# Asking for the spread decays in ScalarE's queue at the end of its step instead of in SyncE's queue behind the returned sums

## What is computed

```python
def step(S, inp):
    qt, kt, vt, at, bt = inp
    err = jnp.einsum('bhij,bhj->bhi', S, kt) - vt
    S = at[..., None] * S - bt[..., None, None] * (err[..., None] * kt[:, :, None, :])
    o = jnp.einsum('bhij,bhj->bhi', S, qt)
    return (S, o)
_, o = lax.scan(step, S0, xs)
```

## Time and profile before

| | |
|---|---|
| median of 3 runs (range) | 7300.07 us (7298.06 to 7325.28) |
| the profiled execution | 7302.33 us, its span 7300.5 us |
| granted TensorE clock, mean | 0.799 |
| busy share of the span: PE, DVE, ACT, POOL | 69%, 74%, 46%, 50% |
| DMA queue q1 (SyncE's): bytes, share of 16 engines | 583.96 MB, 33.1% |
| DMA queue q10 (ScalarE's) | 193.48 MB, 10.7% |
| `db` loads: count, size, median from issue to landing | 124, 1024 KB, 11.7 us |

### The profile page before, as it was taken

The page is one execution under the profiler, slowest core; times in us unless marked ns, Lnnn a source line. Parts: engine busy times, 40 slices in busy tenths (PEclk is TensorE's granted clock), DMA queues, the critical chain, the costliest instruction groups (busy, mean ns, idle before and its releaser), DMA issues. The chain is left out here.

```text
span 7300.5 us, 176124 instructions
## 1 busy us (share of the span) xinstructions
PE 5060.7 (69%) x58695; PEld 3354.2 (46%) x58695; DVE 5418.8 (74%) x16005; ACT 3333.0 (46%) x7234; POOL 3641.1 (50%) x4232
## 2 busy tenths in 40 slices
PE   6666666666666666666667626777777778777777
PEld 4555555545555554555545513333333433334433
DVE  6888888888888888888888855566656566666665
ACT  4454444444544445445544413444444444444444
POOL 3777777777777777777777751111111111111110
PEclk7787777777777778778777757888888888888888
DMA  4666666666666666666666631111111111111111
GB/s 119 159 155 155 154 162 150 151 155 161 152 149 157 155 152 155 157 157 153 151 157 159 148 98 44 44 44 43 43 43 43 43 43 43 43 43 43 43 45 35
DMA packets 1172894, 786.82 MB, mean 108 GB/s; under 512 B 1039923, under 2 KB 1091795, under 8 KB 1157844
## 3 DMA queue, kind: packets, MB, share of 16 engines
q1 hardware_dynamic: 864468, 583.96, 33.1%
q10 hardware_dynamic: 307712, 193.48, 10.7%
HBM read 473.80 MB, written 303.50 MB: 106 GB/s over the span
## 5 line engine op out<-in xcount | busy, mean ns | idle before, releaser
L460 POOL TENSOR_TENSOR qp<-qp,ab 128x512 f32<-128x512 f32 (+7 forms) x1024 | 1027.7, 1004 | 75.3
L465 POOL TENSOR_TENSOR qp<-qp,pt 128x512 f32<-128x512 f32 (+7 forms) x1024 | 869.4, 849 | 85.2 <-issue 4.9
L831 DVE SCALAR_TENSOR_TENSOR p_bank<-y,conv_w,p_bank 128x128 f32<-128x128 f32 x3072 | 827.6, 346 | 96.1 <-issue 45.4
L1688 DVE TENSOR_REDUCE nmax<-w_bank 128x1 f32<-128x512 f32 x1024 | 638.2, 684 | 327.1 <-PE w_bank L1314 317.5
L1269 POOL TENSOR_TENSOR ot<-ot,ln_w 128x1024 f32<-128x1024 f32 x64 | 150.6, 2353 | 1401.3 <-ACT ot L1544 1401.3
L462 POOL TENSOR_TENSOR pt<-qp,vb 128x512 f32<-128x512 f32 (+7 forms) x1024 | 768.6, 751 | 9.2 <-DVE vb L908 9.2
L526 PE MATMUL d_bank<-st 64*32 64x80 f32 x16384 | 512.2, 300 | 347.6 <-issue 340.3
L498 PE MATMUL d_bank<-xd,kt 32*64 32x128 f32 x7936 | 346.3, 322 | 435.2 <-DVE st L849 334.8
L526 PEld LDWEIGHTS d_bank<-st 64*32 64x32 f32 x16384 | 462.4, 148 | 391.9 <-issue 386.2
L590 PEld LDWEIGHTS p_bank<-xnT,wqkv 128*128 128x128 f32 x4096 | 541.4, 213 | 182.6 <-issue 182.6
L590 PE MATMUL p_bank<-xnT,wqkv 128*128 128x128 f32 x4096 | 590.3, 304 | 41.8 <-ACT st L671 34.1
(11 more groups left out here) (219 smaller groups left out, 11504.9 us busy)
## 6 DMA issues: line engine op xcount, KB each, us to landing
db<-decay_dram SPq DMA_DIRECT2D x124, 1024.0 KB, 11.7
prod_dram<-prod ACTq DMA_DIRECT2D x64, 1280.0 KB, 9.1
kp<-prod_dram SPq DMA_DIRECT2D x64, 640.0 KB, 4.9
qp<-prod_dram SPq DMA_DIRECT2D x64, 640.0 KB, 6.7
a_dram<-at ACTq DMA_DIRECT2D x64, 512.0 KB
ab<-a_dram SPq DMA_DIRECT2D x64, 512.0 KB, 5.7
v_dram<-vt ACTq DMA_DIRECT2D x64, 512.0 KB
vb<-v_dram SPq DMA_DIRECT2D x64, 512.0 KB, 5.1
```

The source lines that it names most:

```text
L460: link(nc.gpsimd.tensor_tensor(q, q, ab[:, g, r:r + 1, :].to_broadcast([128, w, DV]), ALU.mult), 1)
L465: link(nc.gpsimd.tensor_tensor(q, q, pt2[:, 0:w], ALU.add))
L831: nc.vector.scalar_tensor_tensor(out=zz, in0=y[:, j % Y_BANKS, i, :, tap:tap + C], scalar=conv_w[:, m, tap:tap + 1], in1=zz, op0=ALU.mult, ...
L1688: nc.vector.tensor_reduce(nmax[:, n:n + 1], bank[:], AX.X, ALU.max, negate=True).then_inc(freed, 1)
```

## The change

The two loads of `db` leave SyncE's slot and become the last thing in ScalarE's slot of the same step, behind `masked_scores(s + 1)`. Their two waits go with them: for the write to `decay_dram` of this step (`dec_wr`), and for VectorE's use of `db` in the step before (`decayed`). What waits for `db` and for the buffers stays as it was.

```diff
@@ SyncE's slot
                     sp.dma_start(xk[:], x_dram[g].rearrange("t b h i -> (b h) t i")).then_inc(xk_in[g], 16)
-                if updates(lo, hi):
-                    sp.wait_ge(*dma_of(dec_wr, n, g, 0))
-                    held(sp, sp_passed)
-                    if due(s):
-                        sp.wait_ge(decayed, s)
-                        held(sp, sp_passed)
-                    for par in range(2):
-                        rows = decay_dram[g][par:par + 1].to_broadcast([64, GB * HP, DV])
-                        sp.dma_start(db[64 * par:64 * par + 64], rows).then_inc(db_in[g], 16)
                 if valid(lo + 4, hi + 4):
@@ ScalarE
+            def spread_decays(s, n, g):
+                act.wait_ge(*dma_of(dec_wr, n, g, 0))
+                if due(s):
+                    act.wait_ge(decayed, s)
+                for par in range(2):
+                    rows = decay_dram[g][par:par + 1].to_broadcast([64, GB * HP, DV])
+                    act.dma_start(db[64 * par:64 * par + 64], rows).then_inc(db_in[g], 16)
+
...
                 if front:
                     masked_scores(s + 1, 1 - g)
+                if updates(lo, hi):
+                    spread_decays(s, n, g)
```

## The result

| | before | after |
|---|---|---|
| median, runs (range) | 7312.67 us, 4 (7298.06 to 7344.51) | 7396.35 us, 4 (7375.65 to 7400.14) |
| the profiled execution | 7302.33 us | 7396.84 us |
| ratio after / before, 95% interval | | 1.0103 (1.0061 to 1.0145) |
| first load of the second half (`wg`) | 4330.32 us | 4412.74 us |

The changed kernel is 1.0% slower. Its recurrence takes 82.4 us more; the other 12 us are in the second half, whose code is the same. The mean granted TensorE clock from 400 to 4200 us was 0.78 before and 0.76 after; the kernel without the loads of `db` (the first experiment) has 0.76 too and is much the fastest, so the clock does not explain the loss. The forecast was 7360 us and slower, with 7325 to 7400 for its likeliest case.

What follows compares the result with a forecast made beforehand. VectorE was taken as the busiest engine, its solve waiting on a chain through TensorE's products, `prod_dram` and `kp`. 27 return steps x 1.7 plus 35 plain steps x 0.4 gave 60 us more: 7360 us, range 7195 to 7450.

Steps and rivals of the forecast that it cites:

- The gap in the products: TensorE's 6.03 us standstill amid the products: instructions waiting behind `db`; moving `db` gives 7.0 us to the chain to `kp`.
- The rival that the stall stays: TensorE's gap in the products is not `db`'s doing and remains: 6.6 us a step, 7709 us; chance 0.14, part or whole.
- `kp` held up by 6.0 to 7.1 us: SyncE's load of `kp`, asked for 2 us after `db` starts, lands that much later, as `v_dram` did: 7.1 us.
- The rival that `kp` is not held up: DMA engines serve `kp` beside `db`, so VectorE's wait for it goes: 7191 us, or 7142 us; chance 0.21.
- VectorE's stall after the branch back: At the convolution (L831) in return steps, VectorE's instructions come late behind `db`: wait grows from 2 to 4 to 6 us.
- The return step: A step in which engines branch back to the loop's start, 27 of 62: VectorE's solve starts 1.7 us later.
- The plain step: A step without the branch back, 35 of 62: `kp` lands about as late as today, 0.4 us more per step.
- The sum: Over the 62 steps with `db`: 27 x 1.7 + 35 x 0.4 = 60 us more, 7360 us against the median.
- Hidden: ScalarE's asks: ScalarE's two asks, 1.9 us ahead of `xnT`, covered by TensorE's 7.11 us wait; without cover at most 66 us.
- `db`'s lateness: `db` lands at about +31 and VectorE uses it at +45.9, so 15 us are spare and nothing is lost.
- The row of `v_dram`: Trace evidence: this write, asked for just after `db` began, landed after 13.4 us instead of 6.3, 7.1 us lost.

Runs made afterwards that it cites:

- the first experiment: The kernel before, without the loads of `db`, its tile filled once with 0.5: 7133.31 us in one run.
- The experiment with `g == 1`: Against the kernel before, the loads of `db` moved to ScalarE's queue in the return steps only: 7336.89 us, ratio 1.0032.
- the experiment with `g == 0`: Against the kernel before, the loads of `db` moved to ScalarE's queue in the plain steps only: 7366.22 us, ratio 1.0062.
- the half spread: The changed kernel with each load of `db` cut to half of its columns, the rest of the tile constant: 7184.11 us in one run.
- the shorter rows: The changed kernel with four loads of 8 KB per partition instead of two of 16 KB, the same bytes: 7380.0 us, ratio 1.0085.
- the split kernel: Against the kernel before, one load of `db` stays in SyncE's queue behind `xk`, the other moves to ScalarE's step end: 7234.55 us, ratio 0.9887.

## Why the prediction was right, and where not

- **The gap in the products is `db`'s and goes.** Right: 319.7 to 29.8 us, and `prod_dram` is asked for at +10.7 where +10.8 was forecast. The rival that the stall stays falls: what grew ahead of the update, 91.0 to 274.6 us, bears the same name in the view but is the wait for `xd`. The Trainium skill ("Runtime: NRT & Kernel Launch", Instruction fetch mechanics) calls the fetch mostly hidden. Where `db` is under way this trace does not agree: 319.7 us of gap in 58 places, against 31.5 us in the kernel without its loads.
- **`kp` held up by 6.0 to 7.1 us.** Right: 6.3 us. The rival that `kp` is not held up falls with this row.
- **VectorE's stall after the branch back grows to 4 to 6 us.** Right: 4.5 us on the mean, 5.1 at most. At +1.36 us a step it is 84 us over 62 steps, as large as the whole loss, but most of it is not paid: with the return steps alone moved, 59 of 70 us come back as shorter waits.
- **The return step, +1.7 us.** Too large. The experiment with `g == 1` moves 31 steps, 27 of them return steps and 4 written out; with the plain step's price below for these 4 it leaves (23 - 4 x 1.5)/27 = 0.6 us (0.2 to 1.1 by the interval). At the solve's start the term was right, 1.7 us on the mean; it stopped there, and behind it the waits for TensorE and `xk` shrink and give most of it back.
- **The plain step, +0.4 us.** The term that was mis-sized: 45/31 = 1.5 us by the experiment with `g == 0`, which moves 31 steps, none of them a return step (1.0 to 2.0 by the interval). At the solve's start the example shows +32.6 against +32.0, 0.6 us, near the forecast, but the mean over the loop's plain steps is 1.2 us, and more is lost behind it, at the update. The step of the prediction that failed is its list of what waits behind `db`: it had `kp` and VectorE's instructions, and not `upd_dram` with the loads of `xd` behind it. `upd_dram` lands 6.3 us later after its ask, and in the plain steps VectorE pays 38 us for it in its wait for TensorE. The row of `v_dram` that priced `kp` would have priced `upd_dram` too.
- **The sum.** 27 x 0.6 + 35 x 1.5 = 69 us instead of 60: two errors of opposite sign, 27 x 1.1 = 30 us too much on one side and 35 x 1.1 = 38 too little on the other. That the total came out near is in part this luck. The loss is 84 us by the medians and 75 by the ratio; of the 36 us between 7360 and 7396 the kernel before accounts for 13, its median having moved from 7300.07 to 7312.67 with a fourth run.
- **Hidden: ScalarE's asks.** Right as far as the half spread and the shorter rows show: with as many asks 212 us are gone, and with twice as many nothing is lost. **`db`'s lateness:** right, the changed kernel has no row of VectorE waiting for `db`; asked for 8 us later there are four such waits, 4.4 us.

## What to carry to other kernels

A large load is paid for by what is asked for in the microseconds behind its start, other queues and instruction fetches included; before moving it, list everything that starts there, each engine's own code too, and follow each item to the wait that it ends. A wait that a view puts down to "issue" is not yet a wait for instructions: look for an instruction packet just ahead of its end, and for a semaphore wait inside it. If every place has some cover and none has enough, don't look for the right place: cut the load and give each place as much as its cover hides, as the split kernel did with 0.9887 of the time at the same bytes. Cut it so that each piece still goes to many partitions: pieces for 64 gained, pieces for 48 and 16 did not.

## What the runs showed that was not expected

The time that `db` costs grows much faster than its bytes: 43 us for the first half and 132 for the second at the old place, 51 and 212 at the new one. A load of 0.75 MB to 48 partitions landed 7.6 us after its ask, one of 1 MB to 64 partitions 7.5 us, as each 16 KB packet took longer; why was not tried. And one word of a view stood for two things: TensorE's 5.5 us of "issue" in the products of each step before were a wait for instructions, its 9.8 us ahead of the update in every second step after are a wait for `xd`.
